# Attention: key maxima taken in pairs over two PSUM banks, two banks for the scores, one probability tile moved from GpSimd's sum to TensorE's

## The chip, the core and the metric

The kernel runs on one NeuronCore of one Trainium2 chip. The metric is the device time of one execution in microseconds (us), as the median of several runs. TensorE does the matrix products and writes PSUM, which has eight banks of 512 float32 values per partition here; VectorE and ScalarE read PSUM; GpSimd does not touch it in this kernel; SyncE issues the transfers.

## What is computed

A block of a vision-language model on four sequences of 512 tokens of width 512: a cross attention of 16 heads of 32 to two contexts (1344 text keys and 257 image keys for each sequence, with a softmax of its own over each, and the two results added), then a mixture-of-experts feed-forward part. The core of the reference for the attention is this:

```python
def attention(q, k, v):
    scores = jnp.einsum('bqhd,bkhd->bhqk', q, k) * scale
    probs = jax.nn.softmax(scores, axis=-1)
    return jnp.einsum('bhqk,bkhd->bqhd', probs, v)

q = rms_norm(linear(x, q_w, q_b), norm_q_w).reshape(B, L, NH, HD)
k = rms_norm(linear(ctx_txt, k_w, k_b), norm_k_w).reshape(B, -1, NH, HD)
v = linear(ctx_txt, v_w, v_b).reshape(B, -1, NH, HD)
k_img = rms_norm(linear(ctx_img, k_img_w, k_img_b), norm_k_img_w).reshape(B, -1, NH, HD)
v_img = linear(ctx_img, v_img_w, v_img_b).reshape(B, -1, NH, HD)
out = attention(q, k_img, v_img) + attention(q, k, v)
```

## The kernel before

The program has three stages: projections (to about 401 us), attention (401 to 1303 us), feed-forward. The change is in the attention, and in the part of the projections that prepares its first group.

**Groups.** The attention runs over 16 groups G (a sequence and four heads each). A group has 13 key tiles `kt` of 128 keys (the last has 65): tiles 0 to 9 are text, tile 10 is half text and half image, tiles 11 and 12 are image. One step of the loop in `pe_attend` handles one key tile. TensorE issues in it

- four scores, one for each head (`score`, line 952), each into one of the banks 2, 3, 4 in turn; ScalarE takes the exponential of each into the tile `P` (line 1077), of which there are four, one for each key tile in flight;
- one weighted sum with the values for the tile two steps back (`weigh`, line 907, bank 6);
- and, for the next group G + 1, some of 64 "maximum units".

**Maxima.** Softmax needs the maximum of each row before its exponential, so the whole product of queries and keys is done twice. A unit (`pe_max_unit`, line 436) is one product of 128 queries by 448 text keys, or by 258 image keys, into one of the banks 0, 1, 5 in turn. VectorE reduces it to one column of maxima (`dve_max_unit`, line 629). The plan `UNITS` says how many of the 64 units of a group stand in each step, and a unit waits only for the reduction three units before it.

**Sums.** The softmax also needs the sum of the exponentials. GpSimd adds text tiles 0 to 7 into `sacc` (seven additions, line 1260), VectorE adds tile 8 (line 1199), and TensorE sums `sacc` and the tiles 9 to 12 over the keys with a matrix of ones (`total`, line 907, bank 7). A tile `P` can be written again only when its weighted sum and its addition or total are done; so the exponentials of tile `kt` wait for the addition of tile `kt - 4`.

**End of a group.** At `kt` 11 TensorE does `text_end` (weighted sums and totals of tiles 9 and 10, four bodies of line 907); at 12 the maxima are transposed (line 441), rounded by ScalarE (line 635) and VectorE, and stored into the rows of the queries; at `kt` 0 and 1 of the next group come the totals and weighted sums of the image tiles (`image`, `image_end`). In groups 5, 9 and 13 four output projections of 12 products each are put into steps 4, 6, 8 and 10.

Each engine runs its instructions in the order in which these functions write them; semaphores carry the waits between engines (`d_ra` counts the reductions, `a_exp` the exponentials, `g_sum` GpSimd's additions).

Of the kernel before, what the change touches and what calls it, by code (L numbers as in the profile page):

```python
# [10 lines left out]
ALU = mybir.AluOpType  # L11
AX = mybir.AxisListType

NB = 4
# [24 lines left out]
def program(nc, ap, ctx):  # L39
# [156 lines left out]
    def units_behind(u):  # L196
        return min(64, 3 * max(0, u - 25))
# [3 lines left out]
    def max_order():  # L201
        blocks = [(j, qt) for j in range(4) for qt in range(4)]
        long = [(c, *x) for c in (0, 1) for x in blocks]
        short = [(c, *x) for c in (2, 3) for x in blocks]
        order = long[:8]
        for i in range(32):
            order.append(short[i])
            if i % 4 != 3:
                order.append(long[8 + i - i // 4])
        return order  # L210

    ORDER_MAX = max_order()

    def rows_ra(G):


        return 64 + 65 * G + 4 * sum(x < G for x in (5, 9, 13))
# [226 lines left out]
    def pe_project():  # L444
# [25 lines left out]
        def units(i, part):  # L470
            nonlocal ra
            first, last = units_behind(i - LAG - 1), units_behind(i - LAG)
            for r in range(first, last):
                if (r - first) != part:
                    continue
                if ra == 0:
                    pe.wait_ge(s_key[0][0], 48)
                    pe.wait_ge(s_qry[0], 48)
                    pe.wait_ge(a_tr, TR4)
                    pe.wait_ge(d_tr, TR4)  # L480
                if ra == 8:
                    pe.wait_ge(s_key[0][1], 144)
                if ra >= 2:
                    pe.wait_ge(d_ra, ra - 1)
                pe_max_unit(0, ra, ra, ra % 2)
                ra += 1
# [3 lines left out]
        for i in range(NIT):  # L490
# [12 lines left out]
            units(i, 0)  # L503
# [5 lines left out]
            units(i, 1)  # L509
# [4 lines left out]
            units(i, 2)  # L514
            if u == 49:
                pe.wait_ge(d_mx, 1)
                pe.wait_ge(d_ra, 64)
                pe_mrow(0)
# [105 lines left out]
    def dve_max_unit(m, ra, bank):  # L624
        c, j, qt = ORDER_MAX[m]
        c0, c1 = CH[c]
        out = mp[:, 4 * qt + j, c:c + 1] if c < 3 else mx[:, qt, 1, j:j + 1]
        dve.wait_ge(p_ra, ra + 1)
        dve.reduce_max(out, ps[:, bank, 0:c1 - c0], AX.X).then_inc(d_ra, 1)  # L629
# [15 lines left out]
    def dve_project():  # L645
# [87 lines left out]
        def units(i, part):  # L733
            first, last = units_behind(i - LAG - 1), units_behind(i - LAG)
            if first + part < last:
                dve_max_unit(first + part, first + part, (first + part) % 2)
# [13 lines left out]
        for i in range(NIT):  # L750
# [17 lines left out]
            units(i, 0)  # L768
# [4 lines left out]
            units(i, 1)  # L773
# [5 lines left out]
            units(i, 2)  # L779
            for k in {0: (4, 5, 6, 7), 1: (8, 9), 2: (10, 11), 3: (12, 13), 4: (14, 15)}.get(i, ()):  # L780
                ln_stats(k)
            if u == 48:
                dve_text_maxima(0, 64)
# [51 lines left out]
    BANKS_RA = (0, 1, 5)  # L835
# [4 lines left out]
    UNITS = (5, 5, 4, 6, 5, 6, 5, 6, 5, 6, 5, 6, 0)  # L840
    PLAN = [[1] * n + [0] * (7 - n) for n in UNITS]

# [8 lines left out]
    def tot_no(G, kt):  # L851
        return 6 * G + {9: 1, 10: 4, 11: 5, 12: 6}[kt]

    TEXT_TOTAL, IMAGE_TOTAL = 3, 6


    def sum_no(G, kt):
        return 7 * G + max(1, kt)
# [57 lines left out]
    def pe_attend():  # L916
        pe.wait_ge(d_mm, NMM)
        ra = 65

        def ra_bank():  # L920
            if ra >= 68:
                pe.wait_ge(d_ra, ra - 2)
            return BANKS_RA[(ra - 65) % 3]

        def units(G, m, n):
            nonlocal ra
            for i in range(m, m + n):
                s = G % 2
                if i == 0:
                    pe.wait_ge(s_key[s][0], 48 * (G // 2 + 1))  # L930
                    pe.wait_ge(s_qry[G % 3], 48 * (G // 3 + 1))
                if i == 8:
                    pe.wait_ge(s_key[s][1], 144 * (G // 2 + 1))
                pe_max_unit(G, i, ra, ra_bank())
                ra += 1

        def score(G, kt, j):
# [34 lines left out]
        def text_end(G):  # L972
            weigh(G, 9, 0, 128, False, False)
            weigh(G, 10, 0, 64, False, True)
            pe.wait_ge(d_img, 2 * G) if G else pe.wait_ge(d_ones, 1)
            total(G, 9, 0, 128, True, False)
# [14 lines left out]
        for step in range(NSTEP):  # L991
            G, kt = divmod(step, NKT)
            more = G + 1 < NG
            plan = PLAN[kt] if more else [0] * 7
            at = sum(map(sum, PLAN[:kt])) if more else 0
            upto = [at + sum(plan[:i]) for i in range(8)]

            def place(i):
                units(G + 1, upto[i], plan[i])
# [5 lines left out]
            if kt == 0:  # L1005
                place(0)
                place(1)
                if G:
                    image(G - 1)
                place(2)  # L1010
                for j in range(4):
                    scored(j)
                    place(3 + j)
# [1104 lines left out]
```

## Time and profile before

| what | value |
|---|---|
| time, median of 3 runs | 1851.11 us (1851.08 to 1859.41) |
| profiled execution: time, span | 1861.8 us, 1860.5 us |
| granted TensorE clock, mean | 0.963 |
| busy: TensorE, VectorE, GpSimd, ScalarE | 96%, 65%, 51%, 44% |

The profile is of one execution; it is 10.7 us above the median of the runs. TensorE's share counts a product as busy until its modelled end, so small waits between products can hide in it. Half of the span is attention. "Idle before" is the time that an engine stood still before a group of instructions, with the instruction that ended the wait.

### The profile page before, as it was taken

How to read it: one execution, taken by the hardware profiler on the slowest of the kernel's cores; microseconds unless marked ns; L12 is line 12 of the kernel's file. 1: busy time of each engine (PE TensorE's matmuls, PEld its weight loads, DVE VectorE, ACT ScalarE, POOL GpSimd, SP SyncE). 2: the span in 40 equal slices, each digit the busy share in tenths (PEclk: the TensorE clock that was granted, in tenths of full speed). 3: DMA queues.
4: the chain of work that ended last, by engine and by line, in shares of the span. 5: the costliest groups of instructions: out<-in, count | busy, mean ns of one | idle time of the engine just before them, and what ended most of it. 6: DMA issues, size and time to landing. Idle time of an engine off the chain costs nothing. (4 is left out here: it accounts for less than half of the span.)

```text
span 1860.5 us, 24747 instructions
## 1 busy us (share of the span) xinstructions
PE 1779.8 (96%) x8822; PEld 1128.5 (61%) x8822; DVE 1200.9 (65%) x2242; ACT 819.4 (44%) x1517; POOL 940.5 (51%) x321
## 2 busy tenths in 40 slices
PE   5999999999999999999999999998899899999999
PEld 4888878863444445444444445432577687888777
DVE  5776676665877777877777787843554445444465
ACT  4443323344555554555455554564222155554221
POOL 3222312125776664776646777465052357767452
PEclk9999999997999999999999999996899999999999
DMA  9456759553443552453453453401141468887432
GB/s 306 152 165 198 225 165 236 167 163 105 128 120 106 134 134 57 121 134 101 125 134 72 112 128 92 118 13 68 39 147 57 142 193 262 270 268 254 157 119 91
DMA packets 185250, 268.73 MB, mean 144 GB/s; under 512 B 24972, under 2 KB 122012, under 8 KB 184612
## 3 DMA queue, kind: packets, MB, share of 16 engines
q1 hardware_dynamic: 180008, 250.36, 46.0%
q0 software_dynamic: 5120, 16.78, 2.6%
q8 instruction: 71, 1.16, 0.3%
q14 instruction: 51, 0.42, 0.1%
HBM read 194.10 MB, written 105.93 MB: 161 GB/s over the span
## 5 line engine op out<-in xcount | busy, mean ns | idle before, releaser
L1077 ACT ACTIVATE P<-ps 128x512 f32<-128x512 f32 (+1 forms) x832 | 442.1, 598 | 361.0 <-PE ps L952 295.1
L629 DVE TENSOR_REDUCE mp<-ps 128x1 f32<-128x448 f32 x768 | 441.3, 615 | 136.5 <-PE ps L436 132.8
L1260 POOL TENSOR_TENSOR sacc<-sacc,P 128x2048 f32<-128x2048 f32 x96 | 441.3, 4597 | 13.9 <-ACT P L1077 0.4
L436 PE MATMUL ps<-Kst,Qst 96*128 96x448 f32 (+1 forms) x1024 | 386.2, 389 | 17.0 <-DVE mp L629 16.6
L952 PE MATMUL ps<-Qst,Kst 100*128 100x512 f32 (+1 forms) x832 | 342.5, 429 | 9.4 <-ACT P L1077 9.3
L436 PEld LDWEIGHTS ps<-Kst,Qst 96*128 96x128 f32 x1024 | 197.2, 193 | 224.7 <-DVE mp L629 132.6
L907 PE MATMUL ps<-P,Vg 128*32 128x512 f32 (+2 forms) x1792 | 254.4, 644 | 6.6 <-issue 6.6
L805 POOL TENSOR_TENSOR cl<-craw,ch 128x1024 fp32r<-128x1024 f32 (+2 forms) x26 | 62.0, 2384 | 286.3 <-ACT ch L541 286.3
L952 PEld LDWEIGHTS ps<-Qst,Kst 100*128 100x128 f32 (+1 forms) x832 | 157.8, 191 | 79.4 <-ACT P L1077 54.4
L49 PE MATMUL ps<-W,ch 128*128 128x512 f32 (+1 forms) x408 | 162.5, 398 | 0.0
L51 PE MATMUL ps<-W,cl 128*128 128x512 f32 (+1 forms) x408 | 159.8, 392 | 0.0
L50 PE MATMUL ps<-W,ch 128*128 128x512 f32 (+1 forms) x408 | 159.4, 391 | 0.0
L2017 POOL TENSOR_TENSOR gul<-gur,guh 128x2048 fp32r<-128x2048 f32 x15 | 69.5, 4631 | 113.3 <-ACT guh L1690 113.3
L629 DVE TENSOR_REDUCE mx<-ps 128x1 f32<-128x258 f32 x256 | 104.3, 418 | 24.0 <-PE ps L436 23.8
L1260 POOL TENSOR_TENSOR sacc<-P 128x2048 f32<-128x2048 f32 x16 | 73.3, 4578 | 79.6 <-ACT P L1077 54.4
L1270 POOL TENSOR_TENSOR oi<-oi,rt 128x512 f32<-128x512 f32 x15 | 19.1, 1276 | 178.9 <-DVE rt L1163 178.9
L907 PEld LDWEIGHTS ps<-P,Vg 128*32 128x32 f32 (+2 forms) x1792 | 39.1, 112 | 92.8 <-issue 64.3
L2017 POOL TENSOR_TENSOR Kst<-gur,Kst 128x2048 fp32r<-128x2048 f32 x15 | 69.4, 4625 | 46.9 <-ACT Kst L1690 46.9
L51 PEld LDWEIGHTS ps<-W,cl 128*128 128x128 f32 (+1 forms) x408 | 75.8, 186 | 17.8
L907 PE MATMUL ps<-P,ones 64*32 64x512 f32 (+2 forms) x640 | 86.3, 626 | 0.0
L50 PEld LDWEIGHTS ps<-W,ch 128*128 128x128 f32 (+1 forms) x408 | 76.0, 186 | 15.3
L49 PEld LDWEIGHTS ps<-W,ch 128*128 128x128 f32 (+1 forms) x408 | 76.0, 186 | 15.3
(229 smaller groups left out, 3043.0 us busy)
## 6 DMA issues: line engine op xcount, KB each, us to landing
gur<-in_w_gate_up SPq DMA_DIRECT2D x23, 1024.0 KB, 7.9
Kst<-KHd SPq DMA_DIRECT2D x32, 640.0 KB, 8.0
Vd<-vf SPq DMA_DIRECT2D x50, 256.0 KB, 2.4
craw<-in_ctxT SPq DMA_DIRECT2D x24, 512.0 KB, 4.4
KHd<-sth SPq DMA_DIRECT2D x24, 512.0 KB, 3.6
KLd<-stl SPq DMA_DIRECT2D x24, 512.0 KB, 4.8
dnr<-in_w_down SPq DMA_DIRECT2D x23, 512.0 KB, 3.9
xg<-Xg SPq DMA_DIRECT2D x23, 512.0 KB, 8.0
```

Of the source, the lines that this page charges most:

```text
L49: pe.matmul(out, ah, bh, start=first, stop=False)
L50: pe.matmul(out, ah, bl, start=False, stop=False)
L51: return pe.matmul(out, al, bh, start=False, stop=last)
L436: pe.matmul(ps[:, bank, 0:c1 - c0], Qst[G % 3][0:96, j, 128 * qt:128 * qt + 128], Kst[G % 2][0:96, j, c0:c1], start=True, stop=True).then_ ...
L629: dve.reduce_max(out, ps[:, bank, 0:c1 - c0], AX.X).then_inc(d_ra, 1)
L805: pool.tensor_tensor(cl[:, n % 3, :, 0:c1 - c0], craw[:, n % 3, :, 0:c1 - c0], ch[:, n % 2, :, 0:c1 - c0].bitcast(F32), ALU.subtract).then ...
L907: ins = pe.matmul(ps[32 * j:32 * j + 32, bank, :], w(j), pt[p0:p1_, j, :], start=first, stop=last, tile_position=(p0, 32 * j))
L952: pe.matmul(ps[:m, 2 + (e - 1) % 3, :], Kst[s][0:100, j, 128 * kt:128 * kt + m], Qst[G % 3][0:100, j, :], start=True, stop=True).then_inc( ...
L1077: act.activation(P[slot(G, kt)][:m, j, :], ps[:m, 2 + (e - 1) % 3, :], ACT.Exp, scale=SCALE).then_inc(a_exp, 1)
L1260: pool.tensor_tensor(sacc[:], (P[slot(G, 0)] if kt == 1 else sacc)[:], P[slot(G, kt)][:], ALU.add).then_inc(g_sum, 1)
L1270: pool.tensor_tensor(oi[:], oi[:], rt, ALU.mult).then_inc(g_oi, 1)
L2017: pool.tensor_tensor(gul[q % 2], gur[raw_slot(q)][:], guh[q % 2].bitcast(F32), ALU.subtract).then_inc(g_gu, 1)
```

## The change

Four things change, and nothing outside of the maxima, the scores and the sums.

1. A maximum **pair** replaces two units: two products go into two neighbouring banks, and one reduction over `[128, 2, columns]` writes two maxima. The 32 pairs of a group use the banks 0 and 1, then 2 and 3, in turn, so a pair waits for the reduction two pairs before it. The plan `PAIRS` spreads them over the steps. In the projections, the pairs of the first group use the banks 0 and 1 alone.
2. Scores go to the banks 4 and 5 alone, so a score waits for the exponential of two scores before.
3. GpSimd adds the tiles 0 to 6 (six additions). Tile 7 gets a `total` on TensorE at `kt` 9; tile 8 stays with VectorE.
4. The order of the pairs, and where in a step they stand.

The diff, cut to its core:

```diff
-    def units_behind(u):
-        return min(64, 3 * max(0, u - 25))
+    def pairs_behind(u):
+        return min(32, (3 * max(0, u - 25) + 1) // 2)
...
+        long = [("L", j, qt) for j in range(4) for qt in range(4)]
+        short = [(kind, j, qt) for kind in "TI" for j in range(4) for qt in (0, 2)]
+        order = long[:6]
+        for i in range(10):
+            order += [short[i], long[6 + i]]
+        return order + short[10:]
...
-    def pe_max_unit(G, m, r, bank):
-        c, j, qt = ORDER_MAX[m]
-        c0, c1 = CH[c]
-        pe.matmul(ps[:, bank, 0:c1 - c0], Qst[G % 3][0:96, j, 128 * qt:128 * qt + 128], Kst[G % 2][0:96, j, c0:c1],
-                  start=True, stop=True).then_inc(p_ra, 1)
+    def pe_max_pair(G, n, bank):
+        for i, (c, j, qt) in enumerate(pair_halves(n)):
+            c0, c1 = CH[c]
+            ins = pe.matmul(ps[:, bank + i, 0:c1 - c0], Qst[G % 3][0:96, j, 128 * qt:128 * qt + 128], Kst[G % 2][0:96, j, c0:c1],
+                            start=True, stop=True)
+        ins.then_inc(p_ra, 1)
...
-        dve.reduce_max(out, ps[:, bank, 0:c1 - c0], AX.X).then_inc(d_ra, 1)
+        dve.tensor_reduce(pair_maxima(n), ps[:, bank:bank + 2, 0:c1 - c0], axis=AX.X, op=ALU.max).then_inc(d_ra, 1)
...
-    BANKS_RA = (0, 1, 5)
-    UNITS = (5, 5, 4, 6, 5, 6, 5, 6, 5, 6, 5, 6, 0)
+    PAIRS = (3, 2, 2, 3, 3, 3, 3, 3, 3, 2, 3, 2, 0)
+    def ra_bank(ra):
+        return 2 * (ra % 2)
...
-            if ra >= 68:
-                pe.wait_ge(d_ra, ra - 2)
-            return BANKS_RA[(ra - 65) % 3]
+            if ra >= 34:
+                pe.wait_ge(d_ra, ra - 1)
+            return ra_bank(ra)
...
-            if e > 3:
-                pe.wait_ge(a_exp, e - 3)
-            pe.matmul(ps[:m, 2 + (e - 1) % 3, :], Kst[s][0:100, j, 128 * kt:128 * kt + m], Qst[G % 3][0:100, j, :],
+            if e > 2:
+                pe.wait_ge(a_exp, e - 2)
+            pe.matmul(ps[:m, 4 + (e - 1) % 2, :], Kst[s][0:100, j, 128 * kt:128 * kt + m], Qst[G % 3][0:100, j, :],
...
+            if kt == 9:
+                pe.wait_ge(d_img, 2 * G) if G else pe.wait_ge(d_ones, 1)
+                total(G, 7, 0, 128, True, False)
...
-                if fk < 8:
+                if fk < 7:
                     act.wait_ge(g_sum, sum_no(G, fk))
...
-                    dve.wait_ge(g_sum, sum_no(G, 7))
+                    dve.wait_ge(g_sum, sum_no(G, 6))
...
-            if G < NG and 2 <= kt < 9:
+            if G < NG and 2 <= kt < 8:
                 add(G, kt - 1)
```

In the listings below, L436 and L629 are a unit's product and reduction before, and L453 and L642 a pair's after; L952 and L969 are a score, L907 and L925 a weighted sum or a total. Steps 5 to 6 on TensorE, from one weighted sum to the next, before:

```order
L907 MATMUL ps<-P,Vg 32x512 x4
L436 MATMUL ps<-Kst,Qst 128x448
L952 MATMUL ps<-Qst,Kst 128x512
L436 MATMUL ps<-Kst,Qst 128x448
L952 MATMUL ps<-Qst,Kst 128x512
L436 MATMUL ps<-Kst,Qst 128x448
L952 MATMUL ps<-Qst,Kst 128x512
L436 MATMUL ps<-Kst,Qst 128x448
L952 MATMUL ps<-Qst,Kst 128x512
L436 MATMUL ps<-Kst,Qst 128x448
L907 MATMUL ps<-P,Vg 32x512 x4
```

and the same stretch of TensorE's order after:

```order
L925 MATMUL ps<-P,Vg 32x512 x4
L969 MATMUL ps<-Qst,Kst 128x512
L453 MATMUL ps<-Kst,Qst 128x448 x2
L969 MATMUL ps<-Qst,Kst 128x512
L453 MATMUL ps<-Kst,Qst 128x448 x2
L969 MATMUL ps<-Qst,Kst 128x512
L453 MATMUL ps<-Kst,Qst 128x448 x2
L969 MATMUL ps<-Qst,Kst 128x512
L925 MATMUL ps<-P,Vg 32x512 x4
```

Three pairs now stand with one score between two of them, and the weighted sum comes after them all and one more score.

VectorE at the end of the maxima of a group, steps 10 and 11 and the transposition that follows, before:

```order
L629 TENSOR_REDUCE mp<-ps 128x1
L629 TENSOR_REDUCE mx<-ps 128x1
L1163 RECIPROCAL rt<-rt 128x128
L1199 TENSOR_TENSOR sacc<-sacc,P 128x2048
L629 TENSOR_REDUCE mp<-ps 128x1
L629 TENSOR_REDUCE mx<-ps 128x1
L629 TENSOR_REDUCE mp<-ps 128x1
L629 TENSOR_REDUCE mx<-ps 128x1
L622 TENSOR_REDUCE mx<-mp 128x4x4
```

and after:

```order
L642 TENSOR_REDUCE mp<-ps 128x2
L642 TENSOR_REDUCE mx<-ps 128x2 x5
L1174 RECIPROCAL rt<-rt 128x128
L1206 TENSOR_TENSOR sacc<-sacc,P 128x2048
L642 TENSOR_REDUCE mx<-ps 128x2
L637 TENSOR_REDUCE mx<-mp 128x4x4
```

Behind VectorE's addition of tile 8 there stood four reductions; now there is one, of a pair of image keys.

TensorE at steps 9 to 11 after, from the weighted sum of step 9, with the new total of tile 7 behind it (before, step 9 had six units and no total):

```order
L925 MATMUL ps<-P,Vg 32x512 x4
L925 MATMUL ps<-P,ones 32x512 x4
L969 MATMUL ps<-Qst,Kst 128x512
L453 MATMUL ps<-Kst,Qst 128x258 x2
L969 MATMUL ps<-Qst,Kst 128x512 x2
L453 MATMUL ps<-Kst,Qst 128x258 x2
L969 MATMUL ps<-Qst,Kst 128x512
L925 MATMUL ps<-P,Vg 32x512 x4
L969 MATMUL ps<-Qst,Kst 128x512
L453 MATMUL ps<-Kst,Qst 128x258 x2
L969 MATMUL ps<-Qst,Kst 128x512
L453 MATMUL ps<-Kst,Qst 128x258 x2
```

In two places two scores now follow each other, or a score follows a short pair, with two banks to go round.

## Rows read from the trace of the kernel before

**Rows 1.** The page: busy time, share of the span and instructions.

```profile
PE 1779.8 (96%) x8822; PEld 1128.5 (61%) x8822; DVE 1200.9 (65%) x2242; ACT 819.4 (44%) x1517; POOL 940.5 (51%) x321
```

**Rows 2.** Groups by form: count, busy us, mean ns, idle time before, releasers.

```profile
L1260 POOL TENSOR_TENSOR sacc<-sacc,P 128x2048 f32<-128x2048 f32 x96 | 441.3, 4597 | 13.9 <-ACT P L1077 0.4
L629 DVE TENSOR_REDUCE mp<-ps 128x1 f32<-128x448 f32 x768 | 441.3, 615 | 136.5 <-PE ps L436 132.8 <-DMA KLd<-stl 2.0
...
L629 DVE TENSOR_REDUCE mx<-ps 128x1 f32<-128x258 f32 x256 | 104.3, 418 | 24.0 <-PE ps L436 23.8
```

**Rows 3.** Timeline of TensorE, group 7, step of six units: start, us, instruction.

```profile
804.92 1.07 PE L907 MATMUL ps<-P,Vg 128*32 128x512 f32 x8
805.91 0.47 PE L436 MATMUL ps<-Kst,Qst 96*128 96x448 f32 x1
806.22 0.40 PE L952 MATMUL ps<-Qst,Kst 100*128 100x512 f32 x1
806.45 0.37 PE L436 MATMUL ps<-Kst,Qst 96*128 96x448 f32 x1
806.66 0.39 PE L952 MATMUL ps<-Qst,Kst 100*128 100x512 f32 x1
...
808.56 1.07 PE L907 MATMUL ps<-P,Vg 128*32 128x512 f32 x8
```

**Rows 4.** Timeline of the same step: VectorE, ScalarE and the weight load.

```profile
806.42 3.28 DVE L629 TENSOR_REDUCE mp<-ps 128x1 f32<-128x448 f32 x6 [0.36 <-PE ps L436]
...
806.65 1.08 ACT L1077 ACTIVATE P<-ps 128x512 f32<-128x512 f32 x2 [1.11 <-PE ps L952]
...
807.10 0.19 PEld L436 LDWEIGHTS ps<-Kst,Qst 96*128 96x128 f32 x1 [0.24 <-DVE mp L629]
```

**Rows 5.** Timeline, group 7, steps 10 to 12: the waits for GpSimd and VectorE.

```profile
829.43 2.06 ACT L1077 ACTIVATE P<-ps 128x512 f32<-128x512 f32 x4 [1.99 <-POOL sacc L1260]
...
831.62 2.06 PE L907 MATMUL ps<-P,Vg 128*32 128x512 f32 x16
...
834.13 1.08 ACT L1077 ACTIVATE P<-ps 128x512 f32<-128x512 f32 x2 [2.64 <-POOL sacc L1260]
834.15 3.28 DVE L1199 TENSOR_TENSOR sacc<-sacc,P 128x2048 f32<-128x2048 f32 x1 [1.03 <-POOL sacc L1260]
...
838.03 0.38 PE L436 MATMUL ps<-Kst,Qst 96*128 96x258 f32 x1 [1.18 <-DVE mp L629]
```

**Rows 6.** Timeline, group 5: the same wait of TensorE.

```profile
733.03 0.38 PE L436 MATMUL ps<-Kst,Qst 96*128 96x258 f32 x1 [0.20 <-DVE mp L629]
```

**Rows 7.** Stretches: length, busy (x) of PE, PEld, DVE, ACT, POOL, granted clock, DMA.

```profile
804.92:827.90 22.98, 22.98 (x124) 12.26 (x123) 19.71 (x41) 14.42 (x28) 21.96 (x6) 1.00 0.14 50
1244.00:1265.00 21.00, 17.75 (x83) 5.76 (x83) 4.66 (x3) 15.48 (x29) 20.43 (x5) 1.00 0.36 131
1265.00:1293.00 28.00, 26.28 (x96) 5.88 (x95) 8.65 (x9) 12.67 (x24) 16.50 (x5) 0.51 0.06 19
831.62:848.26 16.64, 15.46 (x89) 4.33 (x88) 10.98 (x15) 5.87 (x11) 4.95 (x3) 0.79 0.44 90
663.18:678.20 15.02, 13.83 (x89) 4.15 (x89) 11.00 (x15) 5.87 (x11) 4.97 (x3) 0.89 0.49 98
727.58:740.05 12.47, 12.27 (x90) 3.56 (x89) 10.98 (x18) 5.62 (x11) 0.44 (x1) 1.00 0.30 62
```

**Rows 8.** Timeline of TensorE, group 8, steps 0 to 3.

```profile
848.26 0.47 PE L436 MATMUL ps<-Kst,Qst 96*128 96x448 f32 x1
...
859.25 1.06 PE L907 MATMUL ps<-P,Vg 128*32 128x512 f32 x8
```

**Rows 9.** Timeline of TensorE, group 0: its longest wait.

```profile
443.02 0.80 PE L952 MATMUL ps<-Qst,Kst 100*128 100x512 f32 x1 [3.17 <-ACT P L1077]
```

**Rows 10.** Timeline of TensorE, group 15 (no maxima): two waits for the exponentials.

```profile
1259.52 1.48 PE L952 MATMUL ps<-Qst,Kst 100*128 100x512 f32 x3 [0.79 <-ACT P L1077]
...
1264.21 1.48 PE L952 MATMUL ps<-Qst,Kst 100*128 100x512 f32 x3 [1.78 <-ACT P L1077]
```

More of the change, by code:

```diff
@@ L468, in pe_project, with pair @@
         ra = 0
-        def units(i, part):
+        def pair(i, part):
             nonlocal ra
[L472 to L486, printed above, removed]
+            if pairs_behind(i - LAG - 1) + part >= pairs_behind(i - LAG):
+                return
+            if ra == 0:
+                pe.wait_ge(s_key[0][0], 48)
+                pe.wait_ge(s_qry[0], 48)
+                pe.wait_ge(a_tr, TR4)
+                pe.wait_ge(d_tr, TR4)
+            else:
+                pe.wait_ge(d_ra, ra)
+            if ra == PART1:
+                pe.wait_ge(s_key[0][1], 144)
+            pe_max_pair(0, ra, 0)
+            ra += 1
         pe.wait_ge(s_const, 48)
@@ L502, in pe_project @@
                 project_keys(u, 0)
-            units(i, 0)
+            pair(i, 0)
             if 0 <= i - 1 < NT:
@@ L731, in k_low, with pair @@
             dve_transposed(stl[:, n % 2, :, c0:c0 + rows], sth[:, n % 2, :, c0:c0 + rows], rows, tr_no["k", u])
[L733 to L736, printed above, removed]
+        def pair(i, part):
+            n = pairs_behind(i - LAG - 1) + part
+            if n < pairs_behind(i - LAG):
+                dve_max_pair(n, n, 0)
         ln_stats(0)
@@ L767, in dve_project @@
                 q_scale(i)
-            units(i, 0)
+            pair(i, 0)
             if 0 <= u < NU:
@@ L772, in dve_project @@
                 q_low(i - 1)
-            units(i, 1)
             if 0 <= u < NU:
@@ L992, in pe_attend @@
             G, kt = divmod(step, NKT)
[L993 to L996, printed above, removed]
+            pairs = pairs_of(G, kt)
             def place(i):
-                units(G + 1, upto[i], plan[i])
+                if i < len(pairs):
+                    pair(G + 1, pairs[i])
             def scored(j):
@@ L1149, in dve_attend, with reduced @@
         dve.memset(ones[:], 1.0).then_inc(d_ones, 1)
-        ra = 65
-        def units(G, m, n):
+        ra = 33
+        def reduced(G, pairs):
             nonlocal ra
-            for i in range(m, m + n):
-                dve_max_unit(i, ra, BANKS_RA[(ra - 65) % 3])
+            for n in pairs:
+                dve_max_pair(n, ra, ra_bank(ra))
                 ra += 1
@@ L1168, in dve_attend @@
             more = G + 1 < NG
-            plan = PLAN[kt] if more else [0] * 7
-            at = sum(map(sum, PLAN[:kt])) if more else 0
-            upto = [at + sum(plan[:i]) for i in range(8)]
+            pairs = pairs_of(G, kt)
             if step == 2:
@@ L1174, in dve_attend @@
             if kt == 2 and 1 <= G < NG:
-                units(G + 1, at, upto[2] - at)
+                reduced(G + 1, pairs[:1])
                 dve.wait_ge(p_pv, pv_no(pG, 12))
@@ L1197, in dve_attend @@
                     dve.wait_ge(a_exp, exp_no(G, 8, 3))
-                    dve.wait_ge(g_sum, sum_no(G, 7))
+                    dve.wait_ge(g_sum, sum_no(G, 6))
                     dve.tensor_tensor(sacc[:], sacc[:], P[slot(G, 8)][:], ALU.add).then_inc(d_add, 1)
-                units(G + 1, upto[2], sum(plan[2:]))
+                reduced(G + 1, pairs[1:])
                 if more:
@@ L1209, in dve_attend @@
             else:
-                units(G + 1, at, sum(plan))
+                reduced(G + 1, pairs)
             if G in (5, 9, 13) and kt in (4, 6, 8, 10):
-                dve_project_tile((G - 5) // 4, (kt - 4) // 2, ra, BANKS_RA[(ra - 65) % 3])
+                dve_project_tile((G - 5) // 4, (kt - 4) // 2, ra, ra_bank(ra))
                 ra += 1
```

144 lines of the change are left out of this document (69 added, 75 removed).

## The prediction

> **What bounds the kernel now.** I read the page first: TensorE is busy 96% of the span, the others 44% to 65% [rows 1]. So a change pays only where TensorE waits or runs at its lower clock. Then I read the groups by form for the price of a reduction and of an addition [rows 2], and then the timeline of one attention group, since the 96% hides small waits.
>
> The middle of a group (weighted sum of step 3 to that of step 10) takes 22.98 us at full clock [rows 7]. A step of six units takes 808.56 - 804.92 = 3.64 us, one of five about 3.15 us (the same walk with one unit less and no wait). Inside it, the first product behind a weighted sum occupies TensorE for 0.31 us, a score 0.235 us, a unit of 448 keys 0.205 us and the weighted sum 0.99 us [rows 3]. VectorE starts 0.04 us after the end of the product (805.91 + 0.47 to 806.42), and TensorE's next load starts 0.07 us after the reduction (806.42 + 0.615 to 807.10) [rows 2 to 4]. Six reductions in a row take 3.28 us, 0.55 us each, with 0.36 us of waiting before them: six-unit steps are VectorE's, five-unit steps TensorE's.
>
> The end of a group is worse. GpSimd needs seven additions of 4.6 us [rows 2]. They end at 834.1 in group 7, and two engines wait for that: ScalarE 1.99 and 2.64 us for a free probability tile, and VectorE 1.03 us before its addition of 3.28 us [rows 5]. Four reductions are queued behind it, so TensorE waits 1.18 us. Then its clock falls to the lower level: 0.79 over the 16.64 us from `text_end` to the end of the image totals. In group 5, which is longer by the output projections and where GpSimd is early, TensorE waits 0.20 us and the same work takes 12.47 us at clock 1.00 [rows 5 to 7]. Eleven groups show the 1.18 us wait, and all lose the clock, seven as in group 7 and four as in group 4 (15.02 us at 0.89). Three groups (5, 9, 13) show 0.20 us, and none loses it.
>
> **The change part by part.**
>
> *GpSimd's seventh addition goes, tile 7 gets a total.* The chain ends 4.6 us earlier, at about 829.4 in group 7, before `text_end`. VectorE can add tile 8 during `text_end`'s 4 us of TensorE work: reciprocal and addition end some 4.5 us after its start, and only one short reduction is queued behind them, which TensorE issues at 4.3 us. I get no wait for the transposed maxima. So each end of a group should look like that of group 5, 12.4 us. Gain: 7 x (16.64 - 12.47) + 4 x (15.02 - 12.47) = 29.2 + 10.2 = 39.4 us. The new total costs one weighted sum's time, 0.99 us a group, counted below.
>
> *A pair instead of two units.* By the two forms an element costs (615 - 418) / (448 - 258) = 1.04 ns, so a pair of 448 takes 615 + 448 x 1.04 = 1.08 us (bounds: 896 x 1.04 = 0.93 us with no fixed part, and 2 x 615 = 1.23 us with no saving). That frees VectorE, but the pair's banks come free only when all of it is reduced, and only two pairs fit. I walk a step with three pairs, A, B, C, from the end of the weighted sum: score to 0.34; A's products at 0.34 and 0.545; score at 0.75; B at 0.985 and 1.19; score at 1.395; C could start at 1.63. But A's last product ends at 0.545 + 0.37 = 0.915, its reduction runs from 0.955 to 2.035, and C's load starts at 2.105, its product 0.1 later. C waits 0.58 us. Then C to 2.62, score to 2.86, weighted sum from 2.94 to 3.93. Without that wait it is 3.35 us. VectorE is then not the limit: 3 x 1.01 = 3.0 us.
>
> Six intervals of a group (from steps 3 to 9) have a third pair: 5 at 3.93 and one with a short pair at 3.77, together 23.4 us. From 9 to 10 there are the total (0.99) and the scores' new limit, below: 4.07 us. From 10 to `text_end` 3.08 us. Sum 30.6 us. Before, this took 831.62 - 804.92 = 26.70 us [rows 3, 5]. Loss: 3.9 us a group. Groups 1 to 14: +54.6 us. (In groups 5, 9, 13 a projection takes the third turn in four of the steps and waits the same 0.6 to 0.7 us for A.)
>
> *Two banks for the scores.* A score's bank is free again 0.39 (product) + 0.04 + 0.60 + 0.05 = 1.08 us after its start (806.22 and 806.65 show the first part [rows 3, 4]); 1.19 behind a weighted sum. In the middle steps the score two back is 1.3 us or more away: free, as long as pairs stand between. At steps 9, 10 and 12, where pairs are short or missing, a score waits up to 0.4 us; that is in the 4.07, the 3.08 and the 12.4. At steps 0 and 1 it costs 0.45 us and fewer units in steps 1 and 2 give 0.5 us back: the 10.99 us from 848.26 to 859.25 [rows 8] stay 10.9. I set zero.
>
> *Group 0* waits 3.17 us for an exponential that waits for GpSimd, and the score behind it takes 0.80 us where 0.40 is usual: half clock [rows 3, 9]. With the middle 3.9 us later, most of the wait is filled, and its end comes about 7 us earlier. *Group 15* has no maxima: its scores lose 0.5 us in step 0 and 1 in the end, since GpSimd's chain up to tile 6 still sets the pace: +2 us, or down to -8 if the half clock there (0.51 over 28 us [rows 7]) ends sooner. *Projections:* single pair buffer, but between two pairs stand 2.7 us of projection and at least 2.7 us of VectorE work fit: zero, with the 1.08 us reductions ending about 0.6 us ahead of the next pair. At most +5.
>
> Sum: +54.6 - 39.4 - 7 + 2 = **+10 us**. On the profiled execution that is 1861.8 + 10 = 1872 us. The median of the runs is 10.7 us below it (I take it that the clock falls for a shorter time in them, which the change would not repeat), and I put the same +10 us on it: **1861 us**.
>
> Two rules of the Trainium skill bear on this. "VectorE: DVE Perf Modes", section "Rules for kernel authors", says to minimize the number of instructions, since each pays a fixed part; its errata table makes a reduction from PSUM 120 cycles plus one for each element, 0.59 us for 448 and 1.06 us for 896. Rows 2 show 0.615 us, so it agrees; by its figures the wait of C would be 0.56 us and the sum the same within 2 us. It counts VectorE's time, though, and not how long a bank is held.
>
> **The rivals.**
>
> *A. The clock still falls once in each group (0.16).* C's 0.58 us is a new wait in six intervals of a group, and one more late reduction could leave the fall at the end where it is. For it: 1.18 us of waiting did it eleven times, and 1.78 us in group 15 was followed by 0.51. Against it: group 15 ran 21 us at clock 1.00 with TensorE busy 17.75 of 21.00 us and single waits of up to 0.79 us [rows 7, 10]; my step is busy 3.3 of 3.9 us. Price: 16.64 - 12.47 less the 1 us of longer wait is 3.2 us for each, 14 groups: +45 us, 1906 us; half of the groups, 1883 us. It decides if a single wait goes past about 1 us. "TensorE: Matmul & The Clock Gate", section "A second HAM failure mode: psum-queue depth-cycling", tells of this: small idle stretches between groups of products that cycle through PSUM banks make the clock swing. By that rule the time is this rival's; the trace so far shows the swing only behind the longer waits.
>
> *B. The third pair does not wait (0.22).* If the reduction of a pair releases earlier than I walk it, or the products queue better, the middle takes 3.35 us a step. That removes up to 90 waits x 0.58 = 52 us. But then ScalarE's step 10 waits for GpSimd's sixth addition, about 1.2 us a group, 18 us: 1861 - 52 + 18 = 1827 us. For it: six-unit steps are VectorE's, and three pairs need 0.25 us less of it. Against: the unit's turn-round of 1.19 us in rows 3 and 4 leaves no room.
>
> *C. The end does not change (0.08).* GpSimd is early, but VectorE's reciprocal and addition still keep TensorE waiting: the 39 us stay, 1861 + 39 = 1900 us.
>
> **How the numbers follow.** My walk holds with 0.54. Its own range comes from the pair's bounds, (1.23 - 1.08) x 90 = 13.5 us to either side: 1847 to 1875. The whole range leaves out the far ends of A, B and C: 1832 to 1892. A measurement can tell about 0.5% (9 us) from no change. Faster by more than that: B and a little of mine, 0.26. Within: 0.31. Slower by more: half of mine, A and C, 0.43.
>
> **What would show it.** Right: reductions of 1.08 us; TensorE stopped 0.5 to 0.6 us "<- VectorE" before every third pair, middle steps of 3.9 us; no wait over 0.4 us and clock 1.00 in the ends; `text_end` to the last image total 12.4 us; groups of about 53.9 us. Wrong: middle steps of 3.4 us (B), granted clock below 1 in groups 1 to 14 (A), or a wait of 1 us behind VectorE's addition (C).

## The result, and the profile after

| kernel | time, median | ratio to before, 95% interval |
|---|---|---|
| before (4 runs beside it) | 1855.3 us | |
| with the change (4 runs) | 1880.6 us (1873.1 to 1884.7) | 1.013 (1.008 to 1.018) |

The change makes the kernel slower by 1.3%, on the side that had the largest chance (0.43), and 20 us above the forecast of 1861 us. The profiled execution has a span of 1881.8 us, against 1860.5 us: +21.3 us where I had +10.

The page of the kernel after, busy line and the two groups of reductions (x is the count, then busy us, mean ns, idle time before them):

```profile
PE 1772.0 (94%) x8950; PEld 1126.6 (60%) x8950; DVE 1164.0 (62%) x1730; ACT 857.0 (46%) x1517; POOL 866.1 (46%) x305
...
L642 DVE TENSOR_REDUCE mp<-ps 128x2 f32<-128x896 f32 x384 | 403.9, 1084 | 142.6 <-PE ps L453 139.9
...
L642 DVE TENSOR_REDUCE mx<-ps 128x2 f32<-128x516 f32 x128 | 87.4, 693 | 70.7 <-PE ps L453 70.5
```

Every engine but ScalarE is less busy than in [rows 1], and the kernel is slower. VectorE spends 54.3 us less on the maxima (441.3 + 104.3 before [rows 2], 403.9 + 87.4 after), GpSimd 74 us less in all. TensorE's share fell from 96% to 94%: it waits more.

Where it waits is seen in one middle step, group 8 (TensorE, from one weighted sum to the next; it answers to [rows 3]):

```profile
870.98 1.06 PE L925 MATMUL ps<-P,Vg 128*32 128x512 f32 x8
871.98 0.50 PE L969 MATMUL ps<-Qst,Kst 100*128 100x512 f32 x1
872.32 0.57 PE L453 MATMUL ps<-Kst,Qst 96*128 96x448 f32 x2
872.73 0.39 PE L969 MATMUL ps<-Qst,Kst 100*128 100x512 f32 x1
872.96 0.57 PE L453 MATMUL ps<-Kst,Qst 96*128 96x448 f32 x2
873.37 0.39 PE L969 MATMUL ps<-Qst,Kst 100*128 100x512 f32 x1
874.07 0.68 PE L453 MATMUL ps<-Kst,Qst 96*128 96x448 f32 x2 [0.31 <-DVE mp L642]
874.59 0.39 PE L969 MATMUL ps<-Qst,Kst 100*128 100x512 f32 x1
874.91 0.64 PE L925 MATMUL ps<-P,Vg 128*32 128x512 f32 x4
```

The step is 874.91 - 870.98 = 3.93 us. The third pair starts 0.70 us after the score ahead of it, which is a score's 0.23 us and 0.47 us of waiting; the pair then holds TensorE for 0.52 instead of 0.41 us. Together that is the 0.58 us of my walk. The stretches of the group, and the regular end of the group before (length; busy PE, PEld, DVE, ACT, POOL; granted clock; it answers to [rows 7]):

```profile
846.38:859.59 13.21, 12.31 (x87) 3.23 (x86) 8.67 (x10) 5.60 (x11) 1.27 (x1) 1.00 0.55 113
...
870.98:901.59 30.61, 28.39 (x152) 14.59 (x151) 21.69 (x25) 18.70 (x33) 24.56 (x7) 1.00 0.20 59
510.00:1250.00 740.00, 695.47 (x3874) 327.73 (x3867) 516.11 (x580) 414.89 (x725) 406.36 (x117) 1.00 0.42 107
...
792.05:804.30 12.25, 12.02 (x87) 3.26 (x86) 8.67 (x10) 5.60 (x11) 0.67 (x1) 1.00 0.55 113
```

The middle, from the weighted sum of step 3 to `text_end`, takes 30.61 us (26.70 before); the end, from `text_end` to the end of the image totals, 12.25 us in a regular group (16.64 or 15.02 in eleven groups before [rows 7]); the clock stays at its upper level from 510 to 1250 us, where before it fell once in each of eleven groups.

### The profile page after: what moved, and what is told of

It reads as the page before. It is cut to its first block and busy times, and to the rows that moved or that the text cites. A ratio compares the mean times of both kernels' runs of the same rounds, so it can differ in the third digit from the quotient of the medians.

```text
span 1881.8 us, 24459 instructions
## 1 busy us (share of the span) xinstructions
PE 1772.0 (94%) x8950; PEld 1126.6 (60%) x8950; DVE 1164.0 (62%) x1730; ACT 857.0 (46%) x1517; POOL 866.1 (46%) x305
## 3 DMA queue, kind: packets, MB, share of 16 engines
q8 instruction: 72, 1.18, 0.3%
## 5 line engine op out<-in xcount | busy, mean ns | idle before, releaser
L1088 ACT ACTIVATE P<-ps 128x512 f32<-128x512 f32 (+1 forms) x832 | 479.5, 596 | 362.6 <-PE ps L969 340.5
L642 DVE TENSOR_REDUCE mp<-ps 128x2 f32<-128x896 f32 x384 | 403.9, 1084 | 142.6 <-PE ps L453 139.9
L969 PE MATMUL ps<-Qst,Kst 100*128 100x512 f32 (+1 forms) x832 | 367.0, 445 | 21.1 <-ACT P L1088 16.4
L1267 POOL TENSOR_TENSOR sacc<-sacc,P 128x2048 f32<-128x2048 f32 x80 | 367.6, 4595 | 11.3
L453 PE MATMUL ps<-Kst,Qst 96*128 96x448 f32 (+1 forms) x1024 | 284.9, 360 | 27.1 <-DVE mp L642 26.4
L969 PEld LDWEIGHTS ps<-Qst,Kst 100*128 100x128 f32 (+1 forms) x832 | 154.3, 186 | 254.7 <-ACT P L1088 176.8
L925 PE MATMUL ps<-P,Vg 128*32 128x512 f32 (+2 forms) x1792 | 242.6, 616 | 4.6 <-issue 4.6
L453 PEld LDWEIGHTS ps<-Kst,Qst 96*128 96x128 f32 x1024 | 187.2, 191 | 83.7 <-DVE mp L642 60.1
L642 DVE TENSOR_REDUCE mx<-ps 128x2 f32<-128x516 f32 x128 | 87.4, 693 | 70.7 <-PE ps L453 70.5
L925 PE MATMUL ps<-P,ones 128*32 128x512 f32 (+2 forms) x768 | 101.8, 614 | 0.0
L925 PEld LDWEIGHTS ps<-P,Vg 128*32 128x32 f32 (+2 forms) x1792 | 37.7, 108 | 89.2 <-issue 68.1
```

The lines of the kernel that those rows point to most:

```text
L453: ins = pe.matmul(ps[:, bank + i, 0:c1 - c0], Qst[G % 3][0:96, j, 128 * qt:128 * qt + 128], Kst[G % 2][0:96, j, c0:c1], start=True, stop=True)
L642: dve.tensor_reduce(pair_maxima(n), ps[:, bank:bank + 2, 0:c1 - c0], axis=AX.X, op=ALU.max).then_inc(d_ra, 1)
L925: ins = pe.matmul(ps[32 * j:32 * j + 32, bank, :], w(j), pt[p0:p1_, j, :], start=first, stop=last, tile_position=(p0, 32 * j))
L969: pe.matmul(ps[:m, 4 + (e - 1) % 2, :], Kst[s][0:100, j, 128 * kt:128 * kt + m], Qst[G % 3][0:100, j, :], start=True, stop=True).then_inc( ...
L1088: act.activation(P[slot(G, kt)][:m, j, :], ps[:m, 4 + (e - 1) % 2, :], ACT.Exp, scale=SCALE).then_inc(a_exp, 1)
L1267: pool.tensor_tensor(sacc[:], (P[slot(G, 0)] if kt == 1 else sacc)[:], P[slot(G, kt)][:], ALU.add).then_inc(g_sum, 1)
```

## The experiments

"Period" is the distance of two groups, taken from ScalarE's rounding of the maxima in one group to that in the next; "middle" is the stretch above. The ratios are to the kernel before. Seven runs fill a table of the change's parts:

| | scores in 3 banks, single maxima | scores in 2 banks, single maxima | 2 banks, pairs in the change's order | 2 banks, pairs, weighted sum between |
|---|---|---|---|---|
| GpSimd adds seven tiles | before: 1855 to 1857 us | e12: 0.998 | e3: 1.010 | |
| period, middle | 53.3, 26.7 us | 52.1, 27.9 us | 53.4, 29.8 us | |
| tile 7 handed to TensorE | e1: 0.982 | e8: 1.004 | the change: 1.013 | e5: 1.005 |
| period, middle | 50.0, 26.8 us | 53.0, 28.8 us | 54.3, 30.6 us | 53.0, 28.9 us |

### The handover of tile 7 alone (e1)

```diff
-            if G < NG and 2 <= kt < 9:
+            if G < NG and 2 <= kt < 8:
                 add(G, kt - 1)
...
+            if kt == 9:
+                pe.wait_ge(d_img, 2 * G) if G else pe.wait_ge(d_ones, 1)
+                total(G, 7, 0, 128, True, False)
```

> The kernel before, with the handover alone: GpSimd adds six tiles, tile 7 gets a total on TensorE at step 9; units, their three banks and the three score banks stay. My theory (a late GpSimd is what costs the clock at the end of a group): TensorE's 1.18 us wait behind VectorE's addition goes, the granted clock is 1.00 in the ends of groups 1 to 14, text_end to the last image total takes 12.5 us instead of 16.6 or 15.0: 39 us gained, 16 x 0.99 = 16 us lost for the totals, some of it inside the 0.4 us that step 10 waits anyway. About 1830 us, 1820 to 1840. Rival (the clock falls for another reason, or VectorE's reciprocal and addition still hold the reductions): the ends stay at 16.6 us and the time rises by the totals, 1865 to 1875 us.

Measured: 1821.5 us, 0.982 (0.978 to 0.986). With three score banks and single maxima, TensorE has no idle time in the middle and the clock stays up over the groups:

```profile
782.18:808.94 26.76, 26.76 (x149) 14.15 (x149) 21.95 (x46) 16.68 (x33) 24.61 (x7) 1.00 0.22 67
500.00:1190.00 690.00, 682.90 (x3908) 326.62 (x3904) 544.49 (x1003) 388.02 (x731) 406.98 (x117) 1.00 0.44 115
```

The middle is no longer for the added total: 26.76 us with it, 26.70 us without. The step from the weighted sum of step 9 to that of step 10, where the total stands, grew from 3.20 to 4.05 us; the one from there to `text_end` fell from 3.72 to 2.93 us. In it the kernel before has a wait that e1 doesn't have: ScalarE waited 1.99 us for GpSimd [rows 5], and TensorE behind it:

```profile
830.08 0.50 PE L952 MATMUL ps<-Qst,Kst 100*128 100x512 f32 x1 [0.36 <-ACT P L1077]
```

So one part of the change is worth 34 us here, and the others, put on top of it, cost 59.

### Half of each reduction (e2)

```diff
-        dve.tensor_reduce(pair_maxima(n), ps[:, bank:bank + 2, 0:c1 - c0], axis=AX.X, op=ALU.max).then_inc(d_ra, 1)
+        dve.tensor_reduce(pair_maxima(n), ps[:, bank:bank + 2, 0:(c1 - c0) // 2], axis=AX.X, op=ALU.max).then_inc(d_ra, 1)
```

> The changed kernel, with every pair's reduction reading only the first half of the columns of its two banks (224 of 448, 129 of 258): half of the maxima's work is left out, so the maxima are those of half of the keys. The reduction should take 0.62 us instead of 1.08. My theory (the third pair of a step waits because a pair's two banks are held by a 1.08 us reduction): the wait of 0.58 us before every third pair goes, middle steps take 3.35 us instead of 3.93, 52 us gained in all, of which some 18 us come back as a wait for GpSimd's sixth addition at step 10. About 1845 us, 1830 to 1855. Rival (the longer middle comes from the scores' two banks, which a shorter reduction doesn't change): 1875 to 1885 us.

Measured: 1839.2 us, 0.990 (0.986 to 0.994). A reduction takes 0.62 instead of 1.08 us, and the step 3.46 instead of 3.93 us. My walk without any wait has 3.35 us. So all but 0.1 us of the step's loss hangs on how long a reduction holds the pair's banks in this order. The kernel leaves out half of the maxima's work, so it prices the wait and is no way to remove it.

### The change without the handover (e3)

```diff
-            if G < NG and 2 <= kt < 8:
+            if G < NG and 2 <= kt < 9:
                 add(G, kt - 1)
```

and the total of tile 7 is out again.

> The changed kernel with the handover undone: GpSimd adds seven tiles again and there is no total of tile 7; pairs and two score banks stay. Theory H (the handover to TensorE is what keeps the clock at the end of a group): the 1.18 us wait and the lower clock come back, 39 us, less the 16 us of totals: about 1904 us. Theory M (the middle, 3.9 us longer with the pairs' waits, already lets GpSimd finish in time, so the handover is not needed there): text_end starts about 33.2 us after GpSimd's start and its seven additions take 33.2 us, so the wait is under 0.5 us, the clock stays 1.00 and the totals' 16 us are gained: about 1865 us.

Measured: 1874.9 us, 1.010 (1.006 to 1.015), with GpSimd back at seven additions. Theory H fell: no group from 1 to 14 has the wait of 1.18 us or a fall of the clock, though GpSimd's chain is as long as before. The longer middle (29.8 us) covers it. The period is 0.9 us shorter than with the handover, which is the total. In the changed kernel the handover buys nothing in the groups. Theory M had the mechanism, and its time, 1865 us, was 10 us too low: in the profile the groups and group 0 take less, but the time behind the last group's maxima is 632.1 us against 622.9.

### Pairs spread over the step (e4)

Seen from one weighted sum W to the next, with s a score and P a pair, the change has W s P s P s P s. This run has W P ss P ss P in the steps of `kt` 3 to 8:

```diff
+            if 3 <= kt < 9:
+                scored(0)
+                scored(1)
+                place(0)
+                weigh(G, kt - 2, 0, 128, False, False)
+                place(1)
+                scored(2)
+                scored(3)
+                place(2)
+                project(G, kt)
+                continue
```

> The changed kernel with another order on TensorE inside steps 3 to 8: two scores, first pair, weighted sum, second pair, two scores, third pair. Nothing else moves. Every pair is then at least 1.9 us of other work behind the one whose banks it takes. My theory (only the distance between pairs costs): no wait for VectorE in the middle, but the first score of a step now comes 0.88 us behind the one whose bank it takes, and waits 0.2 us: steps of 3.55 us instead of 3.93, 34 us gained, about 1847 us (1838 to 1858). Rival (VectorE's own time for three pairs, with what it does besides, sets the step): steps stay at 3.9 us and the time at 1880.

Measured: 1877.4 us, 1.012 (1.007 to 1.016), steps of 3.92 us: a miss. Behind that equal number stands another wait. The weight loads of TensorE (PEld), which here show a wait before the products do:

```profile
865.71 0.42 PEld L453 LDWEIGHTS ps<-Kst,Qst 96*128 96x128 f32 x2
866.55 0.19 PEld L969 LDWEIGHTS ps<-Qst,Kst 100*128 100x128 f32 x1 [0.42 <-ACT P L1103]
867.04 0.19 PEld L969 LDWEIGHTS ps<-Qst,Kst 100*128 100x128 f32 x1 [0.30 <-ACT P L1103]
```

No pair waits for VectorE any more; two scores wait for ScalarE's exponentials. Four scores now stand with only a pair among them, and two banks hold them. So there are two rings: a pair can't come before the reduction of the pair two before has ended (1.08 us), nor a score before the exponential of the score two before (0.54 us in a row). An order that relieves one crowds the other. Counted through with these durations, the order of the change and that of e4 both give 3.92 us, and W s P s s P s P gives 3.65 to 3.8.

### The weighted sum between second and third pair (e5)

```diff
+            if 3 <= kt < 9:
+                scored(0)
+                place(0)
+                scored(1)
+                place(1)
+                weigh(G, kt - 2, 0, 128, False, False)
+                scored(2)
+                place(2)
+                scored(3)
+                project(G, kt)
+                continue
```

> The changed kernel with one edit: in the steps of key tiles 3 to 8 the order on TensorE is first score, first pair, second score, second pair, weighed sum, third score, third pair, fourth score (the weighed sum stood before the second pair). The run that spread the pairs found a step of 3.92 us again, but there TensorE waited for exponentials (0.43 and 0.30 us before the scores of the next step), no longer for a reduction. Theory, two rings: a pair can't be written before the reduction of the pair two before it has ended (1.08 us each plus the hand-over), a score not before the exponential of the score two before it (0.54 us plus the hand-over); the step is set by whichever ring is crowded in the given order, and the two engines have room on average. Counting both rings with these durations gives 3.92 us for the two orders that ran and 3.65 to 3.8 us for this one, so about 0.23 us less in some 90 steps: 1860 us (1852 to 1869). Rival, VectorE itself: three reductions of 1.08 us with their starts take what a step has, whatever the order: step 3.9, time 1878 to 1883.

Measured: 1865.7 us, 1.005 (1.002 to 1.009), steps of 3.70 us (864.93 to 868.63). What is left of the wait stands before the scores:

```profile
870.16 0.19 PEld L969 LDWEIGHTS ps<-Qst,Kst 100*128 100x128 f32 x1
870.80 0.19 PEld L969 LDWEIGHTS ps<-Qst,Kst 100*128 100x128 f32 x1 [0.45 <-ACT P L1103]
```

### The weighted sum in two halves (e6)

```diff
+                place(0)
+                weigh_half(G, kt - 2, 0)
+                scored(1)
+                place(1)
+                scored(2)
+                weigh_half(G, kt - 2, 1)
+                place(2)
```

where a half is the heads 0 and 1, or 2 and 3.

> The changed kernel, in the steps of key tiles 3 to 8 with the weighed sum cut into two halves of two text heads each: first score, first pair, half a sum, second score, second pair, third score, the other half, third pair, fourth score. The pairs then come at nearly even distances and the scores too. Theory, two rings: neither ring is crowded, the step falls to 3.5 to 3.6 us, TensorE's own work: about 0.36 us less in some 90 steps, 1848 us (1840 to 1858). Rival, VectorE itself: three reductions of 1.08 us and the gaps between them take 3.8 to 3.9 us whatever the order: 1872 to 1883.

Measured: 1927.7 us, 1.040 (1.036 to 1.045). Far outside both. TensorE in one step:

```profile
887.37 1.05 PE L993 MATMUL ps<-P,Vg 128*32 128x512 f32 x4
888.35 0.49 PE L969 MATMUL ps<-Qst,Kst 100*128 100x512 f32 x1
888.68 0.57 PE L453 MATMUL ps<-Kst,Qst 96*128 96x448 f32 x2
889.09 0.40 PE L969 MATMUL ps<-Qst,Kst 100*128 100x512 f32 x1
889.42 1.05 PE L993 MATMUL ps<-P,Vg 128*32 128x512 f32 x4
...
891.88 1.05 PE L993 MATMUL ps<-P,Vg 128*32 128x512 f32 x4
```

Two heads take 1.05 us, as four do (1.06 us): the heads' products run beside each other in strips of the array, and a half is as dear as the whole. The step is 891.88 - 887.37 = 4.51 us with no wait shown on TensorE; less the 0.98 us that a second half costs it is 3.53 us, the 3.5 to 3.6 of the theory. But that subtraction is no test: in a step of 4.51 us three reductions have room by either theory. This run doesn't decide between them; e5, whose step of 3.70 us is below the 3.8 to 3.9 of VectorE itself, and e9 do.

### The first pair of a group later (e7)

```diff
             if kt == 0:
-                place(0)
                 if G:
                     image(G - 1)
+                place(0)
```

> The changed kernel with one edit: at key tile 0 the first pair of the next group's maxima stands behind the image totals of the group before, not ahead of them. In the profile of the changed kernel this pair waits 0.67 us for the key load of that group, which ends only 13 us after its issue, at each of some 14 places, with nothing else for TensorE to do. Theory: the wait is covered by the image totals (2 us), and the step from text_end to the last image total falls from 13.2 to 12.5 us: 14 x 0.67 = 9 us less, 1871 us (1866 to 1876). Rival: the load lands later too, or the reduction of this pair then delays the second pair, and nothing is gained: 1878 to 1883.

Measured: 1888.3 us, 1.019 (1.015 to 1.023), 0.6% worse than the change by the ratios. The premise was false: I had seen the wait in one group and taken it for all. In the profile after it stands once, in group 8, where the load of 640 KB that the pair waits for took 12.2 us from issue to landing; the same load took 10.8 us one group before and 11.4 us one group later, and its median is 11.1 us:

```profile
855.14 0.68 PE L453 MATMUL ps<-Kst,Qst 96*128 96x448 f32 x2 [0.67 <-DMA Kst<-KLd]
```

In all groups the edit costs 0.55 us (54.86 against 54.3 us): three pairs now stand close behind each other in steps 0 and 1, and one waits 0.32 us for VectorE and a score 0.46 us for ScalarE.

### Two score banks: beside the handover (e8), and alone (e12)

```diff
-            if e > 3:
-                pe.wait_ge(a_exp, e - 3)
-            pe.matmul(ps[:m, 2 + (e - 1) % 3, :], Kst[s][0:100, j, 128 * kt:128 * kt + m], Qst[G % 3][0:100, j, :],
+            if e > 2:
+                pe.wait_ge(a_exp, e - 2)
+            pe.matmul(ps[:m, 2 + (e - 1) % 2, :], Kst[s][0:100, j, 128 * kt:128 * kt + m], Qst[G % 3][0:100, j, :],
```

> The kernel before with the handover of the eighth sum and, besides, its scores in two banks instead of three (the maxima single, as before). It prices the loss of the third score bank alone, against the run with the handover only (1821.5 us, a ratio of 0.982). Theory: with single tiles between the scores an exponential of 0.54 us is nearly always done when the score after next comes, so it costs 0 to 0.1 us a step, mostly at the steps whose two last scores stand close: 1826 us, a ratio of 0.984 (0.981 to 0.989). Rival: the third bank was needed, 0.2 us and more in each of 180 steps: 1855 us or more, and the two score banks, not the pairs, are what makes the change slow.

Measured: 1861.8 us, 1.004 (1.001 to 1.007). The rival won: the third score bank is worth 40 us beside the handover. PEld in a step with six single maxima:

```profile
870.59 0.19 PEld L952 LDWEIGHTS ps<-Qst,Kst 100*128 100x128 f32 x1 [0.53 <-ACT P L1079]
870.69 0.19 PEld L436 LDWEIGHTS ps<-Kst,Qst 96*128 96x128 f32 x1
871.07 0.19 PEld L952 LDWEIGHTS ps<-Qst,Kst 100*128 100x128 f32 x1 [0.19 <-ACT P L1079]
```

The middle grows by 2.08 us (28.84 against 26.76), steps 0 and 1 by 0.7 us, the period by 3.0 us.

> The kernel before with its scores in two banks instead of three and nothing else: all seven additions stay on GpSimd. With the handover the same edit cost 40 us (0.982 to 1.004). Theory: GpSimd's chain and TensorE's work run side by side up to the end of a group, so what the middle loses is first taken from the wait at the end: the middle grows by 3.0 us a group, the 1.18 us wait and the low clock behind it disappear as they did with the maxima in pairs and seven additions, and the kernel stays at 1858 us (1850 to 1868). Rival, the two costs add up: 1855.7 + 40 = 1895 us (1885 to 1900).

Measured: 1853.7 us, 0.998 (0.996 to 1.000). The same edit costs nothing when GpSimd keeps its seven additions. The middle grows by 1.2 us, where I had said 3.0, and the end gives more than that back:

```profile
852.30:880.23 27.93, 27.41 (x142) 13.71 (x141) 22.45 (x46) 16.91 (x32) 27.07 (x7) 1.00 0.23 67
880.23:892.71 12.48, 12.44 (x90) 3.65 (x89) 10.49 (x15) 5.98 (x11) 2.50 (x3) 1.00 0.52 104
```

The end is 12.48 us at clock 1.00 with GpSimd's chain unchanged. So in the kernel before GpSimd's chain set a floor under the group, and 1.2 us more in the middle was enough to fill the wait at the end and to spare the fall of the clock.

### The better order with short reductions (e9)

The edits of e5 and e2 together.

> The kernel of the run with the weighed sum between the second and third pair, and each reduction reading half of its columns (the output is then not the reference's, since half of the maxima's work is left out). In the changed kernel's own order the same cut took the step from 3.93 to 3.46 us, since there the reductions held TensorE. Theory, two rings: in this order what is left of the wait (step 3.69, not 3.5) is the scores' ring of two banks, and reductions of 0.62 instead of 1.08 us change next to nothing: step 3.65 to 3.7, periods of the groups 52.5 to 53, time 1860 us (1854 to 1866). Rival: the reductions still hold this order as well: step 3.45 to 3.5, time 1840 to 1846.

Measured: 1855.6 us, 0.998 (0.995 to 1.001). The period is 52.4 us against 53.0, and the steps are 3.66 to 3.68 us, as said: the reductions hardly hold this order. The kernel is 10 us faster than e5 where I had said 5: 0.6 us a period, of which 0.2 us lie in the middle (28.7 against 28.9 us), and 1.1 us in each projection group. The same cut gave 41 us in the change's own order.

### GpSimd's subtractions later: the change (e10), the handover (e11)

```diff
-            if step == 6:
+            if step == 8:
                 for i, src in enumerate((ot2, rt2)):
```

in GpSimd's part: two subtractions (2.38 us each) that make the low part of the output weights, in group 0.

> The changed kernel with one edit: in group 0 GpSimd's two subtractions for the output weights (2.38 us each) stand behind its sixth addition, not ahead of it. Theory: the exponentials at the end of group 0 wait for that addition (ScalarE 2.92 us, TensorE 1.98 us), TensorE's clock is at the lower level for 20.5 us behind it, and this addition is late by the subtractions only. With it 4.8 us earlier there is no wait and no fall: group 0 takes 58 to 59 us instead of 65.05, and the kernel 1874 us (1870 to 1879). Rival: the text's copy of ScalarE now waits for the subtractions instead, and TensorE behind it; nothing is gained: 1879 to 1884.

Measured: 1879.3 us, 1.011 (1.007 to 1.015). Group 0 fell from 65.05 to 56.4 us and group 1 from 56.1 to 54.3, more than I had said, and the kernel hardly moved. Its time lies in the rival's range, but not for the rival's reason: no engine took the wait over. ScalarE in group 0 of the change, and TensorE behind it; the fall of the clock follows for 20.5 us, and in e10 both rows and the fall are gone:

```profile
443.12 1.08 ACT L1088 ACTIVATE P<-ps 128x512 f32<-128x512 f32 x2 [2.92 <-POOL sacc L1267]
...
443.76 0.80 PE L969 MATMUL ps<-Qst,Kst 100*128 100x512 f32 x1 [1.98 <-ACT P L1088]
```

Of these 10 us, 6.7 are lost behind the maxima of the last group, 4.8 of them in group 15 (up to the first output projection behind it), where TensorE now waits 1.82 us and the clock is down for 20.5 us behind it (0.62 over 1290 to 1317 us):

```profile
1291.54 1.28 PE L969 MATMUL ps<-Qst,Kst 100*128 100x512 f32 x2 [1.82 <-ACT P L1088]
```

> The kernel before with the handover of the eighth sum, and the two subtractions behind GpSimd's sixth addition. In the run with the handover alone TensorE waited 3.90 us in group 0 for that addition, and half clock followed for 3.4 us only. Theory: the wait goes, group 0 takes 55 to 56 us instead of 59.2, the rest stays: 1818 us, a ratio of 0.980 (0.976 to 0.984). Rival: ScalarE's text copy takes the wait over: 1821 to 1824 us.

Measured: 1813.6 us, 0.977 (0.973 to 0.981). Group 0 takes 53.5 us instead of 59.2. It has the lowest median of all: three score banks, single maxima, six additions, subtractions later.

## Why the prediction was right, and where it was not

**The middle: right.** The reduction of 1.08 us, three pairs with the third waiting, steps of 3.93 us and 30.6 us for the middle came out within 0.02 us; the walk by turn-round of a bank and not by VectorE's busy time carried it. Rival B (the third pair doesn't wait) is out; e2 shows the step that it would have had, 3.46 us.

**The end: the size right, the cause half right.** 12.25 us against my 12.4. But I credited the 39 us to GpSimd's shorter chain. e3 and e12 keep the long chain and have no wait and no fall at the end either: a middle longer by 3.1 us (e3) or by 1.2 us (e12) covers it. The cost of the middle and the gain of the end are not two terms that can be added: they came out for the change as it is, and would have been wrong for its parts. The handover's own worth showed only where the middle stayed short (e1: 34 us). Rival A (clock still falls) is out: 740 us at clock 1.00, with some 80 waits in them that show 0.3 us and stop TensorE for 0.5 us and more. "TensorE: Matmul & The Clock Gate" of the Trainium skill, section "A second HAM failure mode: psum-queue depth-cycling", says that small idle stretches between groups of products make the clock swing; no run here shows it in the middle of a group.

**Two score banks "set to zero": the term that was mis-sized.** I argued that they were free as long as pairs stood between scores, and that in steps 0 to 2 fewer units pay for them: 10.99 us "stay 10.9". That stretch takes 870.98 - 859.59 = 11.39 us. In four places in it a score's weights wait for ScalarE (before there were two waits of 0.30 us and one of 0.19):

```profile
861.43 0.19 PEld L969 LDWEIGHTS ps<-Qst,Kst 100*128 100x128 f32 x1 [0.38 <-ACT P L1088]
862.07 0.19 PEld L969 LDWEIGHTS ps<-Qst,Kst 100*128 100x128 f32 x1 [0.45 <-ACT P L1088]
...
866.18 0.19 PEld L969 LDWEIGHTS ps<-Qst,Kst 100*128 100x128 f32 x1 [0.45 <-ACT P L1088]
...
867.45 0.19 PEld L969 LDWEIGHTS ps<-Qst,Kst 100*128 100x128 f32 x1 [0.44 <-ACT P L1088]
```

e8, which changes only the score banks against e1, shows the same place: steps 0 and 1 are 0.7 us longer. In the middle steps of the change's order the wait for the pair hides them. With the pairs' wait gone they hold the step at 3.70 us (e5, e9), and with single maxima they cost 0 or 40 us (e12, e8), by whether GpSimd's chain or TensorE sets the group.

**Where the 21 us came from.** The profiled executions, my terms against the measured:

| part | predicted | measured |
|---|---|---|
| group 0 | -7 | +0.4 |
| groups 1 to 14 | +15.2 | +25.6 |
| group 15 and the rest | +2 | -5.4 |
| before the attention | 0 | +0.7 |

*Group 0* was mis-read: I had the wait filled by the longer middle. It shrank only from 3.17 to 1.98 us, and the clock was down for 20.5 us as before. e10 shows what holds it: the sixth addition stands behind two subtractions. *Groups 1 to 14:* 10.4 us more than predicted, in four places. The eleven groups without projections take 0.4 us more than I had (54.3 for 53.9 us), together 4.4 us: that is the 11.39 for 10.9 us of steps 0 to 2, with 0.15 us given back in the end. The projection groups take 66.3 us where my sum leaves 65.2, together 3.3 us. Of each 1.1 us, 0.4 are steps 0 to 2 as in every group, and 0.2 the middle, which grew by 4.1 us in group 5 (38.41 to 42.54) where I had 3.9; the rest I can't place. The first product of an output projection waits for a pair's bank as I had it, "the same 0.6 to 0.7 us". The row, in group 5:

```profile
702.33 0.47 PE L49 MATMUL ps<-Woh,aTh 128*128 128x512 f32 x1 [0.64 <-DVE mp L642]
```

Group 1 has 1.8 us more, which go with the half clock that lasts on from group 0 (e10: 54.34 us without it), and group 8 has 0.9 us, with the one wait for a key load in it. *Group 15 and the rest* gave back 5.4 us, 3.4 of them in group 15, where the half clock lasted 13.7 instead of 27.3 us; I had that as the far end of the term. Over all the runs the time behind the last maxima lay between 620.9 and 633.6 us, with the clock's falls at other places each time, so this term can't be foreseen to better than some 6 us.

The median moved by 25 us and the profiled span by 21; I had put the same +10 on both. Of the 20 us by which the median lies above the forecast, 4 are its base: 1851.1 us in the three runs that I had, 1855.3 in the four of the comparison.

That the time lies in the range is in part luck: group 0 was missed by 7.4 us, and the last group with what follows gave the same 7.4 us back, in a term that varies by some 12 us between runs.

## What to carry to other kernels

A bank ring has a turn-round of its own: write, wait for the last reader, free. Merging two reads into one saves the reader time but holds twice the memory for longer, and here the reader (62% busy) wasn't the bound. Before giving a bank to one ring, count the other ring's turn-round in the actual order of issue; the change, e4 and e5 issue the same instructions in three orders, with steps of 3.93, 3.92 and 3.70 us.

Where two chains run side by side to a common point, cost and gain don't add: the same edit was worth 40 us or nothing. Test each part against the version in which the other chain is already short.

## What the runs showed of the hardware

Two column strips of a 32-column product take as long as four: 1.05 against 1.06 us (e6), so it costs as much to fill half the array. "TensorE: Matmul & The Clock Gate" of the Trainium skill, in "Part 3: Packing small matmuls — row/col tiling", says that products in distinct column groups run concurrently; the trace agrees, and by that rule the price of e6 could have been told beforehand.

The clock didn't follow the length of a wait alone. In group 0 a wait of TensorE of 1.98, 2.90, 3.17 or 3.39 us was followed by 20.5 us at the lower level (after, e2, before, e12), one of 2.81 or 2.98 us by 6.8 (e5, e9), one of 3.90 us by 3.4 (e1), and ones of 0.92, 1.23 and 1.64 us by none (e4, e3, e8), while a wait of about 1.18 us at the ends of eleven groups before was always followed by a fall, for 3.4 or 6.8 us. What decides between them was not tried.
